# Packed biases for all keys in the second half of a layer's queries, and a new order of SP's transfers

## The reference, cut to what matters

```python
attn = einsum('bqd,bkd->bqk', q, k) / sqrt(HD)
rel_bias_h = einsum('bhwc,hkc->bhwk', rq, Rh)      # a bias per query and key row
rel_bias_w = einsum('bhwc,wkc->bhwk', rq, Rw)      # a bias per query and key column
attn = (attn.reshape(b * NH, h, w, h, w) + rel_bias_h[:, :, :, :, None]
        + rel_bias_w[:, :, :, None, :]).reshape(b * NH, hw, hw)
out = einsum('bqk,bkd->bqd', softmax(attn), v)
```

## Time and profile before

| | us |
|---|---|
| median of three runs | 3167.89 (3167.75 to 3173.26) |
| the profiled execution | 3169.72 |
| its span | 3167.9 |
| PE busy in the span | 3109.9 (98%) |
| DVE, ACT, POOL busy | 1713.8, 1229.2, 1097.6 |

### The profile page before, as it was taken

How to read it: one execution, slowest core, us unless ns; L and a number is a source line. 1 busy time by engine, 2 the same in 40 slices (tenths; PEclk the granted TensorE clock), 3 DMA queues, 4 the chain that set the end, 5 groups by cost and what they waited for, 6 DMA issues and landing times.

```text
span 3167.9 us, 48956 instructions
## 1 busy us (share of the span) xinstructions
PE 3109.9 (98%) x20078; PEld 2310.5 (73%) x20078; DVE 1713.8 (54%) x1921; ACT 1229.2 (39%) x1397; POOL 1097.6 (35%) x618
## 2 busy tenths in 40 slices
PE   9999999999999999999999999999999999999999
PEld 6876558887787555888778765688777875568876
DVE  4447745446435784444734587444473457744445
ACT  3346542124234654213423465321343356532232
POOL 0037860025003786003400488500340058840043
PEclk9999999999999999999999999999999999999999
DMA  3212223114321223212531222421153122141113
GB/s 129 94 39 53 48 79 116 41 58 148 133 92 33 50 46 100 97 40 67 171 122 69 39 49 44 129 74 41 60 185 108 67 46 51 40 138 60 41 35 117
DMA packets 193178, 249.38 MB, mean 79 GB/s; under 512 B 123200, under 2 KB 135872, under 8 KB 192960
## 3 DMA queue, kind: packets, MB, share of 16 engines
q1 hardware_dynamic: 191424, 244.69, 26.3%
q10 hardware_dynamic: 1536, 1.57, 0.2%
HBM read 145.50 MB, written 50.33 MB: 62 GB/s over the span
## 4 chain that ended last, share of the span: by engine, by line
PE 80%; POOL 7%; issue 4%; DVE 3%; ACT 3%; DMA 2%; SPq 1%; POOLq 0%; ACTq 0%; DVEq 0%
PE score L1250 14%; PE score L1251 13%; PE score L1252 13%; PE score L1395 13%; PE lot L1452 10%; PE lot L1326 9%; POOL acc L644 6%; PE lot L1469 1%; PE lot L1369 1%; DMA raw<-weights 1%; PE lot L1250 1%; PE lot L1252 1%; PE lot L1251 1%; ACT prob L828 1%; PE lot L1293 1%
## 5 line engine op out<-in xcount | busy, mean ns | idle before, releaser
L644 POOL TENSOR_TENSOR acc<-acc,prob 128x1024 f32<-128x1024 f32 x288 | 714.0, 2479 | 166.9 <-ACT prob L828 132.6
L828 ACT ACTIVATE prob<-score 128x1024 f32<-128x1024 f32 (+3 forms) x576 | 512.3, 910 | 349.9 <-PE score L1395 347.6
L973 DVE TENSOR_REDUCE max_part<-lot 128x1 f32<-128x512 f32 x640 | 411.4, 685 | 126.6 <-PE lot L1326 120.0
L1452 PE MATMUL lot<-prob,v 128*64 128x512 f32 (+4 forms) x2496 | 470.4, 514 | 1.6 <-ACT prob L828 1.6
L644 POOL TENSOR_TENSOR acc<-prob 128x1024 f32<-128x1024 f32 x48 | 125.7, 2619 | 833.0 <-ACT prob L828 833.0
L1395 PE MATMUL score<-q_hi,k_hi 64*128 64x512 f32 (+3 forms) x1152 | 337.9, 400 | 13.2 <-ACT prob L828 11.3
L1326 PE MATMUL lot<-k_hi,q_hi 64*128 64x512 f32 (+2 forms) x1152 | 336.1, 393 | 9.8 <-issue 5.4
L1452 PEld LDWEIGHTS lot<-prob,v 128*64 128x64 f32 x2496 | 156.7, 136 | 232.6 <-issue 193.7
L894 DVE TENSOR_TENSOR w_lo<-raw,w_hi 128x1536 fp32r<-128x1536 f32 x95 | 180.4, 1899 | 248.1 <-ACT w_hi L681 247.6
L1395 PE MATMUL score<-q_lo,k_hi 64*128 64x512 f32 (+3 forms) x1152 | 311.8, 362 | 0.0
L1395 PE MATMUL score<-q_hi,k_lo 64*128 64x512 f32 (+3 forms) x1152 | 311.6, 361 | 0.0
(11 more groups left out here) (131 smaller groups left out, 7069.1 us busy)
## 6 DMA issues: line engine op xcount, KB each, us to landing
raw<-weights SPq DMA_DIRECT2D x96, 768.0 KB, 4.3
g_mem<-g SPq DMA_DIRECT2D x24, 1024.0 KB, 4.4
xin<-x_t SPq DMA_DIRECT2D x24, 512.0 KB, 6.1
xr<-x_t SPq DMA_DIRECT2D x24, 512.0 KB, 5.6
x_mem<-xr SPq DMA_DIRECT2D x24, 512.0 KB, 6.7
xr<-x_mem SPq DMA_DIRECT2D x24, 512.0 KB, 6.0
y_t<-xr SPq DMA_DIRECT2D x24, 512.0 KB, 6.8
recip<-recip SPq DMA_DIRECT2D x368, 32.0 KB, 1.9
```

Source lines behind the costliest of these rows:

```text
L644: nc.gpsimd.tensor_tensor(acc[:, :, a:b], with_, now, ALU.add).then_inc(added, 1)
L828: nc.scalar.activation(prob[:, ug % P_SLOTS, :, 0:b - a], score[:, u % 2, :, 0:b - a], ACT.Exp, scale=SCALE).then_inc(prob_ok, 1)
L973: nc.vector.reduce_max(max_part[:, t, part, h:h + 1], lot[:, (2 * n + h) % 3, :], AX.X)\
L1452: last = nc.tensor.matmul(lot[rows_of(h), bank, x - half * HALF:y - half * HALF], v[:, t, p * 128 + 64 * h:p * 128 + 64 * h + 64], prob[:, ...
```

## The change

Half 1 of the queries gets a second set of packed biases, so that units 8 to 11 (key tiles 0 to 3) are packed too: from unit 8 on in pairs 1 to 5, from unit 10 on in pair 0. Half 0 stays as it is. `packed1` is now twice as large (`[128, 2, 2, HALF]`): its second index is the half of the columns, and the rows are written to both by a broadcast. It lies in weight slot 0 for pairs 0 to 4 and in bias place 0 for pair 5; `packed0` takes the old place of `packed1`.

`pack` falls into parts. `pack_part(f, p, h, part)` issues the six transfers of the hi (0) or lo (1) part, and `pack_last_columns` four more for columns 16 to 31, with a semaphore of their own that PE waits for at unit 12. SP's order for p > 0 becomes: the hi part of `pack(p, 1)`, `spread(p - 1, 1)`, the lo part, the last columns, `load_bias(p + 3)` (p < 3) or chunk 9 (p = 4) or chunk 10 (p = 5), `spread(p, 0)`, `pack(p + 1, 0)`. A load of biases, or of chunk 9, waits until pair p's plain scores are done (`last_plain`: unit 9 in pair 0, unit 3 in the others) and all of its packs have landed.

```diff
-PACKED_FROM = ([6, 12], [4, 12])
+PACKED_FROM = ([6, 10], [4, 8])
...
+def last_plain(p):
+
+    return max(u for u in range(2 * QT) if u < PACKED_FROM[p > 0][u // QT])
...
-    packed = [m.put("packed0", [128, 2, HALF], F32R, at=slot_at[0]),
-              m.put("packed1", [128, 2, HALF], F32R, at=one + 40 * KB)]
+
+    packed0 = m.put("packed0", [128, 2, HALF], F32R, at=one + 40 * KB)
+    packed1 = [m.put(f"packed1{n}", [128, 2, 2, HALF], F32R, at=at)
+               for n, at in enumerate((slot_at[0], bias_at[0]))]
...
+            def bias_used(f, p):
+
+                sp.wait_ge(score_ok, unit_no(f, p, last_plain(p)))
+                for h in range(2):
+                    sp.wait_ge(pack_in[h], packed_no(f, p))
+                sp.wait_ge(columns_in, columns_packed_no(f, p))
...
-                    sp.wait_ge(score_ok, unit_no(f, p - 3, 2 * QT - 1))
-                    sp.wait_ge(pack_in[1], packed_no(f, p - 3))
+                    bias_used(f, p - 3)
...
+            def pack_columns(f, p, h, part, keys, to, done):
+
+                cols = slice(h * HALF, (h + 1) * HALF)
+                for head in range(2):
+                    a = 64 * head + SIDE + BLOCK * (1 - keys)
+                    b = 64 * head + SIDE + BLOCK * part
+                    src = (b_hi, b_lo)[part][SET_OF[0][p]][a:a + BLOCK, cols].bitcast(F32)
+                    sp.dma_start(to[b:b + BLOCK, :, :], src.unsqueeze(1).to_broadcast([BLOCK, 2, HALF]))\
+                        .then_inc(done, 16)
+
+            def pack_rows(f, p, h, part):
+
+
+                cols = slice(h * HALF, (h + 1) * HALF)
+                for head in range(2):
+                    for n in range(2):
+                        a, b = 64 * head + BLOCK * n, 64 * head + BLOCK * part
+                        src = (b_hi, b_lo)[part][SET_OF[0][p]][a:a + BLOCK, cols].bitcast(F32)
+                        if h:
+                            sp.dma_start(packed1[p // LAST][b:b + BLOCK, :, n, :].bitcast(F32),
+                                         src.unsqueeze(1).to_broadcast([BLOCK, 2, HALF]))\
+                                .then_inc(pack_in[1], 16)
+                        else:
+                            sp.dma_start(packed0[b:b + BLOCK, n, :].bitcast(F32), src).then_inc(pack_in[0], 16)
...
-                    pack(f, 0, 0)
-                    pack(f, 0, 1)
+                    for h in range(2):
+                        pack_begins(f, 0, h)
+                        for part in range(2):
+                            pack_part(f, 0, h, part)
+                    pack_last_columns(f, 0)
...
-                    if 0 < p < PAIRS - 2:
-                        load_bias(f, p + 2)
                     if p:
+                        pack_begins(f, p, 1)
+                        pack_part(f, p, 1, 0)
                         spread(f, p - 1, 1)
-                    if p == LAST:
-                        sp.wait_ge(pack_in[1], packed_no(f, LAST - 1))
+                        pack_part(f, p, 1, 1)
+                        pack_last_columns(f, p)
+                    if p < 3:
+                        load_bias(f, p + 3)
+                    elif p == LAST - 1:
+                        bias_used(f, p)
                         weights(f, 9)
-                    if p:
-                        pack(f, p, 1)
-                    if p == LAST:
-                        sp.wait_ge(score_ok, unit_no(f, LAST, QT - 1))
+                    elif p == LAST:
                         weights(f, 10)
                     spread(f, p, 0)
                     if p < LAST:
-                        pack(f, p + 1, 0)
+                        pack_begins(f, p + 1, 0)
+                        for part in range(2):
+                            pack_part(f, p + 1, 0, part)
...
-                is_packed = layer == 0 and t >= QT // 2 and u >= PACKED_FROM[p > 0][half]
+                is_packed = layer == 0 and u >= PACKED_FROM[p > 0][half]
...
+                    if is_packed and u == QT + QT // 2 and k == 3:
+                        pe.wait_ge(columns_in, columns_packed_no(f, p))
```

More of the change, by code:

```diff
@@ L190, in packed_no, with columns_packed_no @@
     return 192 * (f // 2 * PAIRS + p + 1)
+def last_plain(p):
+    return max(u for u in range(2 * QT) if u < PACKED_FROM[p > 0][u // QT])
+def columns_packed_no(f, p):
+    return 64 * (f // 2 * PAIRS + p + 1)
 def first_no(f, p):
@@ L351, in build @@
     half_mm, half_max_ok, wide_ok = sem("half_mm"), sem("half_max_ok"), sem("wide_ok")
-    onehot_in, onehot_ok, pack_in = sem("onehot_in"), sem("onehot_ok"), sems("pack_in", 2)
+    onehot_in, onehot_ok = sem("onehot_in"), sem("onehot_ok")
+    pack_in, columns_in = sems("pack_in", 2), sem("columns_in")
     shifted, b_hi_ok, b_lo_ok = sem("shifted"), sem("b_hi_ok"), sem("b_lo_ok")
@@ L457, in load_bias, with pack_begins @@
                             .then_inc(bias_in[s], 16)
-            def pack(f, p, h):
-                s = SET_OF[0][p]
+            def pack_begins(f, p, h):
                 sp.wait_ge(b_lo_ok, f // 2 * PAIRS + p + 1)
@@ L481, in load_onehot, with pack_part, pack_last_columns @@
+            def pack_part(f, p, h, part):
+                pack_rows(f, p, h, part)
+                to = packed1[p // LAST][:, 0, :, :] if h else packed0[:, :, :]
+                pack_columns(f, p, h, part, 0 if h else 1, to.bitcast(F32), pack_in[h])
+            def pack_last_columns(f, p):
+                for part in range(2):
+                    pack_columns(f, p, 1, part, 1, packed1[p // LAST][:, 1, :, :].bitcast(F32), columns_in)
             def load_onehot(f):
@@ L1391, in score_pass @@
                     elif is_packed:
-                        w, x = key_block[rows_of(h), t % 2, :], packed[half][rows_of(h), int(t % 4 < 2), :]
+                        x = packed1[p // LAST][:, t // 4, :, :] if half else packed0[:, :, :]
+                        w, x = key_block[rows_of(h), t % 2, :], x[rows_of(h), int(t % 4 < 2), :]
                     else:
```

## The result

The changed kernel takes 3182.93 us (median of 8 runs, 3178.53 to 3188.06) against 3171.97 (8 runs, 3167.61 to 3175.88) for the kernel before beside it: 1.0035 times as long, 95% interval [1.0024, 1.0045]. That is slower by 11.0 us where I forecast 8.2 less. The profiled execution took 3185.70 us.

A forecast was written before the change was run, and what follows sets the result against it. PE bounds pairs 0 to 3 and pair 4 up to unit 10, then POOL. Saved passes 15.6 - 3.8 unit 8 waits - 3.6 last pair = 8.2 us, 3167.9 to 3159.7; range 3151.5 to 3166.5.

The forecast's parts named there:

- The last pair: Pair 5, unit 8: packs land late, PE starts 3.3 us late, POOL ends later; 3.6 us lost over four images.
- C: Rival, chance 0.08: six packs ahead of the spread delay reciprocals, so VectorE's reductions hold PE; +12 us, 3172.
- D: Rival, chance 0.07: POOL's chain in pairs 4 and 5 grows by one stretched add an image; +5 us, 3164.7.
- Would another engine refuse the faster pace? I cost them at nothing.: Shorter packed units: VectorE's 1.29 us per maximum fits under 1.38, POOL and ScalarE have idle time; cost 0.
- B: Rival, chance 0.15: in half 1, POOL's adds or VectorE's reductions and late packs eat half or more; about 3165.
- I take 3.8 us of PE waiting at unit 8: Unit 8, pairs 1 to 4: late packs at seven of sixteen places 2.8 us, SP pauses 1 us.
- a pass is 0.23 us: PE's packed units: each saves one 0.23 us pass; 17 on the path an image, four images, 15.6 us.
- the wider row copies cost what column copies cost: SP's queue: a 64 KB row copy with broadcast takes 0.63 us to issue, like a column pack.
- POOL's part from pair 4's unit 10 on: From pair 4's unit 10 on POOL is the bound; five of the 22 packed units an image save nothing.
- the moved loads and the new order at no cost: Bias loads behind pack(p, 1), weight chunks 9 and 10, last columns: hidden in SP's idle time or early enough, cost 0.

The follow-up runs named there:

- Run 2: Changed kernel with three float32 products of ones ahead of the wait for packed in half 1 of pair 5; 3170.33 us, ratio 0.9993.
- Run 4: Changed kernel with half 1 packed from unit 9 in pairs 1 to 4 and from unit 12 in pair 5; 3168.62 us, ratio 0.9992.
- 5: Run 4 with the second maximum behind unit 9 moved behind unit 3; 3172.49 us, ratio 1.0002.
- 7: Kernel before the change with only the second maximum behind unit 9 moved behind unit 3; 3183.18 us, ratio 1.0034.
- run 8: run 1 with row copies that only units 10 and 11 read issued last in each part, on their own semaphore; 3159.81 us, ratio 0.9958.
- run 3: Changed kernel with half 1 packed from unit 10 in pairs 1 to 4 and from unit 12 in pair 5; 3169.05 us, ratio 0.9995.
- run 1: Changed kernel with half 1 of pair 5 packed from unit 12, as before the change; 3172.35 us, ratio 0.9995.
- run 9: Changed kernel, pair 5 still packed from unit 8, with row copies only units 10 and 11 read issued last, own semaphore; 3165.91 us, ratio 0.9979.

## Why the prediction was wrong

**"The last pair", the term that failed.** The lateness was right: 3.3 us predicted, 3.35 in image 0. Its price was not. I carried it to POOL as 0.85 us, with every pass after the stand at 0.23 us; 3.75 was lost in image 0, and about 13.3 against 3.6 in all (0.85, 1.65 and twice 0.5 add up to 3.5). What I left out is the clock, which fell to 0.51 at the stand and stretched unit 9 by 4 x 0.20 and the values by 1.62, some 2.4 us. Run 2, which adds three products there and so keeps the clock, gives 12.6 us back, 9.6 of it in pair 5, and the 3.7 us that pair 5 then costs are what I had forecast: the sum was right for a full clock, and the clock was missing from it. Even the upper end of that term, 4 x 2.5 = 10, was below what was measured. Of the rivals, C ended on the right side but by another mechanism: PE's waits for maxima only went from 2.5 to 3.6 us, so the reciprocals were not held back enough, and what PE stood for were packs. D's longer adds did not come either: POOL is busy 1086.1 us instead of 1097.6, and the add that took 3.92 us before took 2.35.

**"Would another engine refuse the faster pace? I cost them at nothing."** It was wrong at one unit of sixteen. I set one maximum, 1.29 us of VectorE, against a unit of 1.38, and overlooked that unit 9 has a second one behind it. The whole cost is the 3.7 us of unit 9's passes. Run 4 shows the pass gaining nothing without any wait for packed, and 5 against 7 shows it paying 0.22 in each place (3.6 us over the 16) once the extra maximum is elsewhere. B had the mechanism, at one unit only.

**"I take 3.8 us of PE waiting at unit 8" was too little by half:** 7.5. The margins that I read at sixteen places were from -0.7 to +0.5 us, so a little lateness in SP's queue turns many of them at once. The list of waits shows only 2.7 us at these places (17.2 less the 14.5 of pair 5), since it counts idle time from the modelled end of a matmul, 0.16 us after the next could have started, and leaves out the short ones. The starts show the rest. In pair 3 of image 0 the pass `q_hi,k_lo` of the same head starts at 346.60, so the pass of packed was due at 346.83:

```profile
346.60 0.39 PE L1443 MATMUL score<-q_hi,k_lo 64*128 64x512 f32 x1
...
347.78 0.50 PE L1443 MATMUL score<-packed,key_block 64*128 64x512 f32 x1 [0.57 <-DMA packed<-b_lo]
```

It is 0.95 us late where the list has 0.57, and the next pass comes 0.10 us later than usual behind it. Over the sixteen places the passes of packed are 6.5 us late in sum, and these restarts add about 1. In run 8 the same sum is 0.01 us. Run 8 takes two transfers, about 1.3 us, from in front of the landing and gets all of it back, so it hangs on when the packs land.

**Right:** a pass is 0.23 us (3.6 to 3.7 us over the 16 places for unit 10 and for unit 11 of pairs 1 to 4; 0.91 us over the four images for unit 10 and for unit 11 of pair 0); the wider row copies cost what column copies cost; POOL's part from pair 4's unit 10 on; the moved loads and the new order at no cost (run 3). The issues of packed after (ns, min/median/max):

```profile
L505 SPq DMA_DIRECT2D packed<-b_lo x96: 585/606/2002, 214.9 to 2797.1; - x96
...
L493 SPq DMA_DIRECT2D packed<-b_hi x144: 586/598/1917, 205.5 to 2800.9; - x144
```

Run 8 is 11.4 us below its own runs of before, more than the 8.2 of the forecast: 13 passes an image with no waits instead of 17 with 7.4 us of them.

**Open:** the clock also falls for 3.4 us or more at places that vary between kernels and between runs, and most of the scatter goes with it: of the 35 runs of the kernel before beside 1 to 4, those at a mean clock of 0.998 took 3167.5 to 3170.0 us and those at 0.995 took 3175.9 to 3180.0. The profiled execution of the changed kernel is one of its slower ones (0.991; those at 0.994 and 0.995 took 3178.5 to 3180.2). The kernel before has such stretches too:

```profile
1024.50:1027.90 3.40, 3.40 (x19) 2.96 (x18) 2.86 (x4) 1.53 (x2) 0.91 (x2) 0.50 0.12 29
```

This one came after PE had stood for 1.36 us before 1024.02. A stand of that length is at the same place of every image, and the clock fell behind it in images 1 to 3 and not in image 0. Why it costs the clock at one time and not at another I did not settle, nor why run 1 had more of them than run 8, which differs in the order of SP's transfers alone. They are a large part of the 12.5 us between the medians of 1 and 8. The profiled executions differ by 15.7 us: 6.4 in layer 0's attention, 4.8 of it at unit 8, and 6.6 in the first 200 us, before any of the change's work. At a mean clock of 0.998 run 1 took 3164.4 and 3165.8 us and run 8 3158.3 to 3160.4, so some 6 us are left for the packs. Nor did I try to give unit 9's second maximum a place where VectorE is free; unit 3 is not one.

## What to carry to other kernels

A wait of TensorE is not priced by its length alone: where its granted clock falls with it, the stretch behind can cost more than the wait did (here 9.6 us of the 13.3). Look at the granted clock behind each stand, and compare runs at like mean clock where the change itself does not move it. Where a transfer must be late, give TensorE something to do meanwhile, or leave the old path in that one place. Before paying for a faster unit, look at every unit it applies to for what another engine does in that one, not in the usual one; and when a consumer waits for a batch of transfers, order the batch by who reads it first and count the two parts apart.

## What the runs showed of the hardware

- The four stands of 3.35 to 4.28 us in the changed kernel each came with a clock at half, over 6.9 us at 0.51 in image 0; those of 1.86, 2.32 and 2.45 us in run 9 did not; one of 3.06 us was followed by a window of 8 us at 0.79. The kernel before has 3.4 us at half behind a stand of 1.36 us in three images and not in the fourth, so the length of a stand alone does not decide it.
- Three float32 matmuls of ones (six in the trace, 2.85 us), whose result nobody reads, kept the clock at 1.00 over the same wait and made the kernel 12.6 us faster.
- The row copies, now 64 KB with a broadcast, cost SP 0.593 to 0.606 us an issue (medians of the two parts), the column copies of that size and form 0.598, and the row copies of 32 KB before 0.589; a tail of issues of 1.9 to 2.0 us stayed.
- The list of waits understates short waits of TensorE: passes that were 6.5 us late in sum stand in it with 2.7.
- Most of these kernels' runs spread over 8 to 16 us, those of run 8 over 6: a single run cannot show a gain of 0.2%.
